# Cross-attention, a batch in flight: scores moved behind the next values, keys in a score bank

## The reference, cut to what matters

```
xn     = layernorm(x)                               # 64 x 32 x 256
q      = xn @ Wq ; k = ctx @ Wk ; v = ctx @ Wv      # ctx: 64 x 257 x 256
logits = q . k per head (16 heads of 16) * scale + bias
out    = softmax(logits over the 257 keys) . v
x      = x + out @ Wo
```

## Time and profile before

| | |
|---|---|
| median of 3 runs | 3512.74 us (3510.6 to 3521.19) |
| the profiled execution, first to last instruction | 3512.3 us |
| TensorE busy | 3266.2 us, 93% |
| VectorE, ScalarE, GpSimd busy | 63%, 41%, 29% |
| these three stages, by the first and the last start of their maxima (L1099) | 529.4 to 952.6, 1771.3 to 2192.5, 2729.7 to 3142.7 us |

### The profile page before, as it was taken

The page is one execution under the profiler, slowest core; times in us unless marked ns, Lnnn a source line. Parts: engine busy times, 40 slices in busy tenths (PEclk is TensorE's granted clock), DMA queues, the critical chain, the costliest instruction groups (busy, mean ns, idle before and its releaser), DMA issues. The chain is left out here.

```text
span 3512.3 us, 105565 instructions
## 1 busy us (share of the span) xinstructions
PE 3266.2 (93%) x39150; PEld 2585.9 (74%) x39150; DVE 2217.2 (63%) x7505; ACT 1454.0 (41%) x4212; POOL 1003.2 (29%) x1620
## 2 busy tenths in 40 slices
PE   7978999999987999999999999888999999988799
PEld 6767887777766888888877777765666777767576
DVE  4767226666667988889556666763334666668455
ACT  2334335555532333333255555541111555556222
POOL 0112113333243444444323333442110111112421
PEclk9989999999997999999999999979999999999699
DMA  6643332222112000000011111042112111110323
GB/s 222 212 177 154 115 100 58 57 57 54 62 40 103 3 2 2 2 2 2 13 44 45 43 43 44 2 146 98 46 46 69 43 39 39 39 35 2 114 79 113
DMA packets 145872, 225.26 MB, mean 64 GB/s; under 512 B 14216, under 2 KB 121480, under 8 KB 143816
## 3 DMA queue, kind: packets, MB, share of 16 engines
q1 hardware_dynamic: 138816, 203.16, 18.4%
q0 software_dynamic: 6816, 18.69, 1.5%
HBM read 201.03 MB, written 38.74 MB: 68 GB/s over the span
## 5 line engine op out<-in xcount | busy, mean ns | idle before, releaser
L3303 POOL TENSOR_TENSOR l1fu_second_weighed<-l1fu_second,l1fu_parts 128x256 bf16<-128x256 bf16 x384 | 273.0, 739 | 342.9 <-DVE l1fu_second L3544 336.0
L3355 PEld LDWEIGHTS l1fu_ps_u<-l1f_xnT_all,l1f_key_in 128*128 128x128 f32 x2048 | 252.5, 195 | 17.4 <-issue 11.2
L3355 PE MATMUL l1fu_ps_u<-l1f_xnT_all,l1f_key_in 128*128 (+1 forms) x2048 | 255.0, 279 | 8.7 <-issue 5.5
L3366 PE MATMUL l1fu_ps_y<-l1f_key_out,l1fu_units 128*128 128x256 f32 x1024 | 250.6, 389 | 1.7 <-DVE l1fu_units L3552 1.7
L3366 PEld LDWEIGHTS l1fu_ps_y<-l1f_key_out,l1fu_units 128*128 128x128 f32 x1024 | 185.7, 190 | 33.3 <-issue 6.0
L3417 ACT COPY l1fu_plane<-l1fu_ps_p 128x512 f32<-128x512 f32 x128 | 75.1, 586 | 249.4 <-PE l1fu_ps_p L3345 249.4
L3539 DVE TENSOR_TENSOR l1fu_first<-l1fu_index,l1fu_counted 128x1024 bf16<-128x1024 bf16 x128 | 165.0, 1289 | 20.3 <-PE l1fu_ps_p L3345 17.6
L3425 ACT ACTIVATE l1fu_units<-l1fu_ps_u 128x512 f32<-128x512 f32 x128 | 76.6, 599 | 150.6 <-PE l1fu_ps_y L3366 138.5
L3011 DVE TENSOR_TENSOR l2f_hidden<-l2f_hidden,l2f_ps_u 128x512 f32<-128x512 f32 x55 | 37.8, 688 | 148.9 <-PE l2f_ps_u L2755 139.1
L1020 ACT ACTIVATE l2x_scores<-l2x_scores,l2x_minus_big 128x257 f32<-128x257 f32 x256 | 129.2, 513 | 2.5 <-DVE l2x_minus_big L1104 2.4
L1020 ACT ACTIVATE l1x_scores<-l1x_scores,l1x_minus_big 128x257 f32<-128x257 f32 x256 | 129.2, 513 | 2.1 <-DVE l1x_minus_big L1104 2.1
(11 more groups left out here) (747 smaller groups left out, 8379.8 us busy)
## 6 DMA issues: line engine op xcount, KB each, us to landing
rows_by_expert<-in_zeros_dram SPq DMA_DIRECT2D x1, 17544.0 KB
l0x_ctxT<-in_ctx_T_dram SPq DMA_DIRECT2D x32, 514.0 KB, 5.2
l0x_ctx_rows<-in_ctx_dram SPq DMA_DIRECT2D x64, 256.0 KB, 3.4
l0f_w<-in_L_ffn_w_dram SPq DMA_DIRECT2D x16, 1024.0 KB, 5.1
l1x_ctx_sb<-in_ctx_T_dram SPq DMA_DIRECT2D x64, 256.0 KB, 2.8
l2x_ctx_sb<-in_ctx_T_dram SPq DMA_DIRECT2D x64, 256.0 KB, 2.8
l3x_ctx_sb<-in_ctx_T_dram SPq DMA_DIRECT2D x64, 256.0 KB, 2.8
l1x_mask_raw<-in_mask_int_dram SPq DMA_DIRECT2D x16, 514.0 KB, 3.9
```

The lines of the kernel that those rows point to most:

```text
L3303: last = nc.gpsimd.tensor_tensor(second_weighed[:, k % 2, part], second[:, k % 2], parts[:, 1 - par, part, TC * k:TC * k + TC].unsqueeze(2 ...
L3355: last = nc.tensor.matmul(ps_u[:, k % 2, j, :], key_in[:, c, JS * k + j, :], xnT_all[:, c, bass.ts(tile, P)], start=(c == 0), stop=(c == C ...
L3366: last = nc.tensor.matmul(ps_y, units[:, k, j, :], key_out[:, JS * k + j, :], start=(k + j == 0), stop=(k == K - 1 and j == JS - 1))
```

## The change

Four edits, all in `cross_attention`:

- On TensorE `values(t+3)` comes ahead of `score(t+2)`, so the scores stand between the values and the outputs.
- The keys go to the first bank of `ps_s` and no longer to `ps_kv`. They wait until VectorE has read that bank for batch t+1 (a new semaphore, `bank_read`, which the first of the four maxima increments); the scores wait until ScalarE has copied the keys out. The values keep `ps_kv` and wait for VectorE's copy of the values of t+2.
- On VectorE `keep_values(t+3)` comes ahead of `maxima(t+2)`.
- On GpSimd the tail keys and the bias of turn 1 come behind the shares of that turn.

```diff
-            def keys(at, before, dst=ps_kv):
+            def keys(at, scored, dst=ps_keys):
                 b, n = at
                 pe.wait_ge(per_batch["ctx_loaded"][b], n * 16)
-                if before:
-                    pe.wait_ge(per_batch["v_kept"][before[0]], before[1])
+                if scored:
+                    pe.wait_ge(per_batch["bank_read"][scored[0]], scored[1])
...
-            def values(at, dst=ps_kv):
+            def values(at, before, dst=ps_kv):
                 b, n = at
-                if dst is ps_kv:
-                    pe.wait_ge(per_batch["kT_ready"][b], n)
+                if before:
+                    pe.wait_ge(per_batch["v_kept"][before[0]], before[1])
...
-            def score(at, before):
+            def score(at, before, projected):
...
+                if projected:
+
+                    pe.wait_ge(per_batch["kT_ready"][projected[0]], projected[1])
...
                     turn_shares(now, before)
+                    if ahead3:
+                        values(ahead3, ahead2)
                     if ahead2:
-                        score(ahead2, ahead)
-                    if ahead3:
-                        values(ahead3)
+                        score(ahead2, ahead, ahead3)
                     outputs(now)
...
+                    if r == 0:
+                        last.then_inc(per_batch["bank_read"][b], 1)
...
                     keep_probs(now, before2, is_draining(t, last))
+                    if ahead3:
+                        keep_values(ahead3)
                     if ahead2:
                         maxima(ahead2)
-                    if ahead3:
-                        keep_values(ahead3)
                     if ahead:
                         inverse(ahead)
```

More of the change, by code:

```diff
@@ L644, in cross_attention @@
         per_batch = {k: [nc.alloc_semaphore(f"{tag}_{k}{b}") for b in range(BT)] for k in
-                     """ctx_loaded k_ready kT_ready v_ready v_kept scores_ready biased_ready max_ready
+                     """ctx_loaded k_ready kT_ready v_ready v_kept scores_ready bank_read biased_ready max_ready
                      exp_ready inv_ready share_ready tail_share_ready probs_turned_1 probs_turned_2 probsT_1 probsT_2
@@ L684, in cross_attention @@
         first_values = (halves(ps_s[:, 1]), halves(ps_s[:, 3]), halves(ps_p[:].rearrange("p r k -> p (r k)")))
+        ps_keys = halves(ps_s[:, 0])
         ps_p2 = ps_kv[:].rearrange("p a (r k) -> p (a r) k", r=2)
@@ L782, in turn @@
                             layer_norm_root(pool, nc, s, n + 1, mean[:], rstd[:], core.table("minus_half"))
-                    if not last and t == 1:
-                        put_tail_keys(i + 1, n + 1)
-                        mask_bias(n + 1)
                     if not first and t == 0:
@@ L789, in turn @@
                         shares(ahead, before)
+                    if not last and t == 1:
+                        put_tail_keys(i + 1, n + 1)
+                        mask_bias(n + 1)
             layer_norm_root(pool, nc, s, 1, mean[:], rstd[:], core.table("minus_half"))
@@ L936, in turn @@
                     if ahead3:
-                        keys(ahead3, ahead2)
+                        keys(ahead3, ahead)
                     if not first and t == 0:
@@ L954, in _ @@
             keys((0, 1), None, first_keys[0])
-            values((0, 1), first_values[0])
+            values((0, 1), None, first_values[0])
             turn_xn(1)
@@ L958, in _ @@
             queries(1)
-            values((1, 1), first_values[1])
+            values((1, 1), None, first_values[1])
             keys((2, 1), None, first_keys[2])
             pe.wait_ge(s["tail_values"], 1)
-            values((2, 1), first_values[2])
+            values((2, 1), None, first_values[2])
             for b in range(2):
@@ L965, in _ @@
                 pe.wait_ge(per_batch["v_kept"][b], 1)
-            score((0, 1), None)
-            score((1, 1), (0, 1))
+            score((0, 1), None, None)
+            score((1, 1), (0, 1), None)
             all_tiles(pe, turn)
@@ L1001, in keep_tail_values, with keep_keys @@
                 nc.scalar.copy(v_tail[:].rearrange("p c b -> p (c b)"), ps_vt).then_inc(s["tail_values"], 1)
-            def keep_keys(at, src=ps_kv):
+            def keep_keys(at, src=ps_keys):
                 b, n = at
```

## The result

The changed kernel takes 3531.9 us, the median of 14 runs, against 3512.59 for 14 runs of the kernel before beside them: a ratio of 1.0052, 95% interval 1.004 to 1.0064. (13 of the 14 lie between 3524.5 and 3541.8; a single one of 13530.84 us stands far off and moves the median by less than 0.5 us.) Its profiled execution spans 3524.3 us, 12.0 more than that of before. The forecast was 3530, slower by 0.5%.

The account below looks back on a forecast made before the run. TensorE, busy 356 of 360 us, was taken to set the pace. From a span of 3512.3 us, -35.7 - 17.6 + 21.6 + 45.5 + 3.5 = +17.3 gave 3529.6, forecast as 3530 us; range 3508 to 3548.

Parts of the forecast that it names:

- The switch of tile shape: TensorE, scores behind values: three shape switches per turn instead of four, 0.195 us in each of 183 turns, -35.7 us.
- The rival of no drain between two small shapes: TensorE, scores straight into outputs: no switch cost there, 18.3 us more gain, 3511 us, no change; chance 0.08.
- The bias: GpSimd, mask bias after batch 2's shares: turn 2 loses a 0.59 us wait, 15 tiles, two masked stages, -17.6 us.
- The output product: TensorE, turn 0: the product waits for oT, a stall of 0.48 us in 15 tiles of three stages, +21.6 us.
- The transposes of x: TensorE, turn 1: they wait for the normalised x, a stall of 1.01 us, 15 tiles, three stages, +45.5 us.
- The keys' new wait: TensorE, keys into the first score bank: just fits, 0 us; rival that it binds, +9 to +27 us, chance 0.17.
- The last tile: Last tile, turn 1: scores start 2.55 us into the turn instead of 1.43; 1.1 to 1.2 per stage, +3.5 us.
- The rival in which VectorE isn't late: VectorE's chain behind the scores 1.0 us shorter, so neither TensorE stall appears: 3462.5 us; chance 0.09.

Follow-up runs that it names:

- e3: Changed kernel with both the output product moved behind the shares and the transposes of x behind the values: 3463.5 us, ratio 0.9859 to the kernel before.
- e4: Kernel before with only the GpSimd edit, tail keys and mask bias behind the shares in turn 1: 3486.43 us, ratio 0.9932.
- e5: Changed kernel with the VectorE edit undone, maxima ahead of the copy of the values again: 3580.67 us, ratio 1.0194 to the kernel before.
- e2: Changed kernel with the output product behind the shares in turn 0, and VectorE's addition behind its copy of the weights: 3508.06 us, ratio 0.9998.
- e1: Changed kernel with the transposes of x behind the values in turn 1, and ScalarE's copy of them behind the exponentials: 3490.84 us, ratio 0.9945.
- e6: Changed kernel with the keys waiting for all four maxima instead of the first: 3603.5 us, ratio 1.0263 to the kernel before.

## Why the prediction held, step by step

**The switch of tile shape** (-35.7). Turn 3, in which no other term lies, went from 6.22 to 6.03, and turn 0 from 6.96 to 6.76 in e3: 0.19 to 0.195, as counted. The rival of no drain between two small shapes is out: the scores' recorded end, 720.93 + 0.69 = 721.62, lies 0.07 past the outputs' start, as at every switch of the earlier trace rows and in the earlier trace rows, and not 0.16 as where the shape stays. The Trainium skill, "TensorEngine Tiling (Array Packing)", section Tiling Modes, Key Properties, says that a change of the tiling mode drains the array; the trace agrees, by this 0.07.

**The bias** (-17.6). Turn 2 of the masked stages is 5.85, the same as in the third; e4 alone gives 18.1. In the changed kernel the bias comes in time for the maxima that need it, with the 0.3 us that the forecast gave it:

```profile
738.94 3.72 POOL L755 TENSOR_SCALAR l1x_bias<-l1x_mask_raw 128x1028 f32<-128x1028 int32 x1
...
742.28 0.69 PE L870 MATMUL l1x_ps_s<-l1x_kT,l1x_q_by_half 32*64 32x257 f32 x16
...
743.31 0.43 DVE L1103 CUSTOM_DVE_ANT_0 l1x_scores<-l1x_ps_s,l1x_bias 128x257 f32<-128x257 f32 x1 [0.23 <-PE l1x_ps_s L870]
```

It ends at 742.66, the scores at 742.97. e5 shows this room used up.

**The output product** (+21.6). From the scores' end to `oT` it is 724.80 - 721.62 = 3.18, the figure that the last tile had given. The forecast's 0.48 is there, but in two places, which "a wait of 0.4 to 0.5" did not say: the group starts 0.38 later, and takes 1.13 instead of 1.03, since its first load is exposed. The bracket shows only 0.22, because the modelled end of the keys runs 0.16 on. Turn 0 grew by 0.29, which is 0.48 less 0.195; e2 takes the 0.48 back.

**The transposes of x** (+45.5). 0.99 by starts and 0.02 or 0.03 in the group's length; turn 1 grew by 0.82, which is 1.01 less 0.195, and e1 takes back 1.01. In the third stage both stalls are 0.03 shorter.

**The keys' new wait** (0, with up to 27 us and a chance of 0.17 beside it). They start 0.49 into the turn as before, behind no wait. The forecast reckoned a room of 0.01 us, and that is what the changed kernel has in turn 1, from the first maximum to the load of the keys:

```profile
729.34 0.43 DVE L1103 CUSTOM_DVE_ANT_0 l1x_scores<-l1x_ps_s,l1x_bias 128x257 f32<-128x257 f32 x1 [0.23 <-PE l1x_ps_s L870]
...
729.89 1.60 PEld L842 LDWEIGHTS l1x_ps_s<-l1x_ctx_sb,weights 128*128 128x128 f32 x8
```

The maximum ends at 729.77 and the load begins 0.12 later, where 0.11 is what it takes from VectorE to TensorE; e6 gives the same 0.01. It held, but by a hair: e6 shows what missing it costs.

**The last tile** (+3.5). The place that was named is there: in turn 1 the shares wait for the weighing, and the scores start 950.02 - 947.52 = 2.50 into the turn, where 2.55 was forecast and 1.43 was before.

```profile
947.52 0.66 PE L882 MATMUL l1x_ps_p<-const,l1x_scores 128*128 128x128 f32 x4
...
949.65 0.33 PE L903 MATMUL l1x_ps_o<-const,l1x_tail_share 128*128 128x128 f32 x1 [1.04 <-DVE l1x_lastT L1148]
...
950.02 0.69 PE L870 MATMUL l1x_ps_s<-l1x_kT,l1x_q_by_half 32*64 32x257 f32 x16
```

Of this turn 1 keeps 0.94 (3.67 before, now 4.61). Turn 0 is 0.12 longer than in the loop (the step from turn 3 to turn 0 takes 0.12 less there, so that the product meets `oT` 0.12 earlier), and turn 2 is 3.71 against 3.64. Together 1.13 per stage; that this meets the 1.1 to 1.2 is partly luck, since the forecast put all of it in turn 1.

**The sum.** The stages grew by 15.2 us by the starts of the turns: 2.2, 2.7 and 10.3, where 3, 3 and 12 were forecast. Three things make the difference: the 0.03 at each stall of the third stage; turn 1 of the first tile, which is 7.72 and not 8.13, so that its stall is 0.4 short of the 1.01 that all 15 tiles were given; and the first turn of a stage, in which the first loads come in and which takes 7.2 to 9.5 us from one execution to the next. The end of the first stage adds 1.1, for a reason given at the end. That is 16.3 against a forecast of 17.3. The profiled span shows 12.0, with 4.3 less outside the stages and this end, and the medians 19.3 (14 to 22 by the interval): both agree with the 16.3 within the scatter of the rest.

The rival in which VectorE isn't late fell with the first two lines of the waits. But its number, 3462.5, is what e3 measures, 3463.5: it priced the change without its two stalls, and e3 removes them not by a faster VectorE but by asking for its results later.

## What to carry to other kernels

A step that is moved later in one engine's turn moves everything behind it on the engines that follow, and the readers of those results may stand early in the next turn: count, for each reader, when it is due and when the chain now delivers. If a move gains on the bounding engine and stalls it elsewhere, move the readers as well, past work that is ready; here that turned +0.5% into -1.4%. And a stall is read from starts and from the length of the group behind it, since the bracket leaves out what a modelled end covers.

## What was not expected of the hardware

In the last tile, where TensorE waits often, its granted clock dropped in some stages and not in others. The windows of the changed kernel, at the end of its first stage, and of the kernel before at the same place (columns as in the earlier trace rows):

```profile
950.00:954.00 4.00, 2.87 (x59) 1.81 (x58) 3.65 (x17) 3.06 (x11) 0.81 (x2) 1.00 0.00 0
954.00:958.00 4.00, 2.82 (x42) 2.46 (x42) 1.90 (x7) 2.28 (x8) 0.77 (x2) 0.74 0.01 4
```

```profile
950.00:954.00 4.00, 3.06 (x63) 2.12 (x62) 3.56 (x17) 3.19 (x12) 1.04 (x3) 1.00 0.00 0
954.00:958.00 4.00, 2.26 (x44) 1.68 (x44) 2.52 (x9) 3.12 (x12) 0.78 (x2) 1.00 0.01 4
```

The clock stands between its two levels in the second line of the first: for part of that stretch it is 1.2 GHz and not 2.4. From the last group of transposes to the output product the stage then takes 5.03 us, where it takes 3.88 in the kernel before and in the changed kernel's other two stages. The same tail is 4.7 to 4.9 us long in one stage of e1, two of e2 and one of e6, and 3.88 or 3.89 in all others; in the kernel before and e4 it is that in all six. In e5 the clock fell earlier in the last tile, in two stages: from 972 to 976 us, in the first of them, the granted clock is 0.57, and turns 1 and 2 take 5.46 and 4.31 us, where they take 5.06 and 3.69 in the third stage. One of the two drops of e2 began as early. TensorE's busy time ahead of the drop (2.87 of 4 us) is little different from that of the kernel before (3.06), so these rows don't tell what decides it. It costs 0.7 to 1.6 us for each such stage, and nothing was tried against it.
